# One ring of eight buffers for statistics and streamed units, spread in proportion to VectorE's passes

## The chip, the cores and the metric

The kernel runs on 1 core of one Trainium2 chip. The metric is device time in microseconds (us). TensorE is PE in the profile (its weight loads PEld), VectorE is DVE, ScalarE is ACT, GpSimd is POOL, SyncE is SP. "SPq" and "ACTq" are DMAs issued from the SP and ACT queues.

## The reference, cut to what matters

The input is one image of 16 channels of 2048 x 2048 floats. Both layers normalize over groups of two channels; the first adds a masked depthwise convolution, the second a bias that depends on row minus column and on the channel.

```
x = x + conv(gn(x))       # conv: 6 x 11 taps per channel, lower triangle (row >= column) in and out
x = x + (gn(x) + bias)    # bias[c, i, j] = table[i - j + 2047, c]; table from a small MLP
gn(v): mean and variance over 2 channels x 2048 x 2048, (v - m) / sqrt(var + 1e-5)
```

Above the diagonal the first layer changes nothing, so there the output is an affine function of the input plus the bias.

## The kernel before

A channel is four bands of 512 rows (128 partitions x 4 rows). A group is two channels; there are 8. The convolution runs over 90 tiles of a group (`NT` = 90), of which 42 touch the diagonal and take one more pass. The program is a pipeline of stages, one per group: in stage s, phase A takes the statistics of group s, phase B convolves group s-1, and phase C normalizes and stores group s-2. Stage 0 takes the first group's statistics alone, stage 1 has A and B, stages 2 to 7 have all three (stage 7 reads no statistics ahead for a next group), stage 8 has B and C, and stage 9 has C alone. Within a stage each engine walks the positions n = 0 to 89, one tile each, in an order written out by hand; an item "at position n" is issued between the tile work of n and of n + 1. SP has no tile work: it goes through its loads in the order of their positions, as fast as the waits of each let it.

Per position PE transposes a tile (L1117) and convolves one (L1131, 36 matmuls); ACT copies the transposed tile as f16 (L611), normalizes a later tile (L599) and sums squares of finished pieces (L631); DVE writes the f16 remainder (`split_lo`, L751), masks a diagonal tile (L764) and adds the result to x (`evict`, L766); POOL masks (L1031) and copies the halo columns (L1057, L1046). ACT and DVE work in order, so a late transfer for one item holds the tile work behind it.

Work around the tiles:

- **Statistics units ("a").** 58 units of 512 KB a group (`A_STREAM`) are loaded from x by SP (L488) into `abuf`, 4 buffers, and read by DVE: two `bn_stats` passes a unit (`stream_stats`, L779). Load `a` waits for `a_done` of unit `a - 4`. Loads lead their use by 2 positions.
- **Streamed units ("u").** 36 units of 512 KB a group (`STREAM`) are loaded from x, or from the output where the first layer's result was spilled there, by SP (L508) into `ubuf`, 4 buffers. Most are scaled by ACT (`scale_stream`, L658) and get the bias from POOL (`add_bias`, L1066); 13 take one DVE pass instead (`finish_stream`, L949). ACT issues the store (`store_stream`, L665) one position after a DVE unit and two after a POOL unit, and load `u` waits for the landing of store `u - 4`.
- **Kept blocks.** 14 parts of a group, in two halves each, stay in SBUF between B and C; DVE finishes them in place (L940), ACT stores them (L646), and SP loads the next group's into the same place (L524) once the store has landed.
- **Transit blocks** (`band`, 1 MB each) of bands 0 and 1 are loaded (L534), convolved and spilled (L638).
- The bias rows are loaded twice a group; the load for the second channel (position 43) waits for all units of the first.

A planner, `plan`, sets the positions. It books the fixed transfers in `traffic` (megabytes per position), and `spread` deals units over a window so that fixed and streamed traffic together come to the same level at each position, times `weight(n)`: 1 for statistics; `U_WEIGHT` for the u units: 1.8 below position 10, 1.5 above 82, else 1. After that a load is pushed back if its buffer would not be free, and with it the use:

```
p.u_load.append(max(at - 2, p.u_store[u - NUB] + 1) if u >= NUB else 0)
p.u.append(min(max(at, p.u_load[u] + 1, p.u[-1] if u else 0), hi))
p.a_load.append(max(at, p.a[a - NAB] + 1) if a >= NAB else at)
```

Of the kernel before, what the change touches and what calls it, by code (L numbers as in the profile page):

```python
# [25 lines left out]
def preact_conv_kernel(nc, x, wflip, w1, b1, w2, b2, w3, b3, out):  # L26
# [89 lines left out]
    def a_loads(g, a):  # L116

        of = lambda count: -(-(count - a % NAB) // NAB)
        return a // NAB + 1 + (of(NA0) + of(NA) * (g - 1) if g else 0)

# [3 lines left out]
    NAB, NUB = 4, 4  # L124
# [8 lines left out]

    U_WEIGHT = lambda n: 1.8 if n < 10 else 1.5 if n > 82 else 1.0
# [48 lines left out]
    def a_items(positions, s, n, do_a, do_next):  # L183

        if s == 0:
            return [(1, a) for a, at in enumerate(positions) if n == NT - 1 and at < 0]
        now = [(s, a) for a, at in enumerate(positions) if at == n]
        return (now if do_a else []) + [(s + 1, a) for a, at in enumerate(positions) if do_next and at == n - NT]

    def plan(do_a, do_b, do_c, on_dve=None):  # L190

        traffic = [0.0] * (NT + 8)
        lap = do_a and do_b and do_c

        def book(at, megabytes, over=2):
            for i in range(over):
                traffic[at + i] += megabytes / over
        for blk in KEPT:
            if do_c:
                book(kept_pos[blk][0] + 1, 1.0)  # L200
# [10 lines left out]
        def spread(count, megabytes, lo, hi, weight):  # L211
# [18 lines left out]
        p.u_load, p.u, p.on_dve, p.u_store, p.a_load, p.a = [], [], [], [], [], []  # L230
        if do_c:
            for c, (lo, hi) in enumerate(U_WINDOW):
                for at in spread(NU // 2, 1.0, lo, hi, U_WEIGHT if do_a else lambda n: 1.0):
                    u = len(p.u)
                    p.u_load.append(max(at - 2, p.u_store[u - NUB] + 1) if u >= NUB else 0)
                    p.u.append(min(max(at, p.u_load[u] + 1, p.u[-1] if u else 0), hi))
                    p.on_dve.append(on_dve[u] if on_dve else U_ON_DVE(p.u[u], u))
                    p.u_store.append(min(p.u[u] + (1 if p.on_dve[u] else 2), NT - 1))
                    book(p.u_load[u], 0.5, 1)
                    book(p.u_store[u], 0.5, 1)  # L240
        if lap:
            for at in spread(NA, 0.5, A_LO, A_END - 2, lambda n: 1.0):
                a = len(p.a)
                p.a_load.append(max(at, p.a[a - NAB] + 1) if a >= NAB else at)
                p.a.append(min(p.a_load[a] + 2, A_END))
        else:
            p.a_load, p.a = STEADY.a_load, STEADY.a
        return p
# [6 lines left out]
    N_DVE, N_POOL = u_before[1][NU], u_before[0][NU]  # L255

# [10 lines left out]
    with ctx:  # L267
# [15 lines left out]
        abuf = sb("abuf", [P, NAB, 2, BW], f32)  # L283
        ubuf = sb("ubuf", [P, NUB, 2, BW], f32)
# [38 lines left out]
        pos_in = ubuf[0:DIM, :, :, :].rearrange("p a b c -> p (a b c)")  # L323
# [21 lines left out]
        a_loaded = [sem(f"a_loaded{i}") for i in range(NAB)]  # L345
# [9 lines left out]
        u_loaded = [sem(f"u_loaded{i}") for i in range(NUB)]  # L355
# [3 lines left out]
        u_stored = [sem(f"u_stored{i}") for i in range(NUB)]  # L359
# [88 lines left out]
        def _(sp):  # L448
            def load_first():

                for i, (kind, of) in enumerate(FIRST_LOADS):
# [4 lines left out]
                    elif kind == "stream":  # L456
                        wait_alone(sp, a_done, max(0, of - NAB + 1))
                        sp.dma_start(unit_of(abuf, of % NAB, A_FIRST[of]), part(xv[A_FIRST[of][0], A_FIRST[of][1]], A_FIRST[of])
                                     ).then_inc(a_loaded[of % NAB], 16)
# [17 lines left out]
            def stage(s, do_a, do_b, do_c, do_next):  # L477
                p, ga, gb, gc = plan(do_a, do_b, do_c, on_dve), s, s - 1, s - 2
# [4 lines left out]
                for n in range(NT):  # L483
                    for g, a in a_items(p.a_load, s, n, do_a, do_next):
                        u = A_STREAM[a]

                        wait_alone(sp, a_done, a_base(g) + (a - NAB + 1 if a >= NAB else 0))
                        sp.dma_start(unit_of(abuf, a % NAB, u), part(xv[chan(g, u[0]), u[1]], u)  # L488
                                     ).then_inc(a_loaded[a % NAB], 16)
# [4 lines left out]
                    if do_a and s > 0:  # L494
                        if n == W_LOAD[0]:
                            load_taps(ga, 0)
                        load_transit(ga, 0, n)
                    if do_c:
                        for u in range(NU):
                            if p.u_load[u] == n:  # L500
                                c, b, q, nq = STREAM[u][:4]
                                wait_alone(sp, u_stored[u % NUB], 16 * (gc * (NU // NUB) + u // NUB))
                                spilled = q <= b
                                if spilled:
                                    for i in range(nq):
                                        wait_alone(sp, x1_spilled[(b, q + i)], 16 * (chan(gc, c) + 1))
                                src = (ov if spilled else xv)[chan(gc, c), b]
                                sp.dma_start(unit_of(ubuf, u % NUB, STREAM[u]), part(src, STREAM[u])  # L508
                                             ).then_inc(u_loaded[u % NUB], 16)
                        if n == BIAS_LOAD[1]:  # L510
                            load_bias(gc, 1)
                    if do_b:
# [4 lines left out]
                        if n == NEXT_BIAS_LOAD:  # L517
                            load_bias(gb, 0)

# [40 lines left out]
        def _(act):  # L560
# [93 lines left out]
            def scale_stream(g, u):  # L654

                v = ubuf[:, u % NUB, :, :]
                act.wait_ge(u_loaded[u % NUB], 16 * (g * (NU // NUB) + u // NUB + 1))
# [3 lines left out]
            def store_stream(g, u):  # L661
# [3 lines left out]
                act.dma_start(part(ov[chan(g, c), b], STREAM[u]), unit_of(ubuf, u % NUB, STREAM[u])  # L665
                              ).then_inc(u_stored[u % NUB], 16)

            def stage(s, do_a, do_b, do_c, do_next):
                p, ga, gb, gc = plan(do_a, do_b, do_c, on_dve), s, s - 1, s - 2
                for n in range(NT):  # L670
# [29 lines left out]
                    if do_c:  # L700
# [7 lines left out]
                        for u in range(NU):  # L708
                            if p.u[u] == n and not on_dve[u]:
                                scale_stream(gc, u)  # L710
# [4 lines left out]
                        for u in range(NU):  # L715
                            if p.u_store[u] == n:
                                store_stream(gc, u)
# [5 lines left out]
            for i in range(NUB):  # L723
                act.wait_ge(u_stored[i], 16 * G * (NU // NUB))
# [5 lines left out]
        def _(dve):  # L730
# [51 lines left out]
            def stream_stats(g, a):  # L782
                if a == 0:
                    wait(dve, s1_chain, 11 * g - 8)
                dve.wait_ge(a_loaded[a % NAB], 16 * a_loads(g, a))
                take_stats((A_STREAM if g else A_FIRST)[a], lambda q, r: abuf[:, a % NAB, q + r, :]).then_inc(a_done, 1)
# [156 lines left out]
            def finish_stream(g, u):  # L943
# [3 lines left out]
                dve.wait_ge(u_loaded[u % NUB], 16 * (g * (NU // NUB) + u // NUB + 1))  # L947
                v = unit_of(ubuf, u % NUB, STREAM[u])
# [11 lines left out]
            def stage(s, do_a, do_b, do_c, do_next):  # L960
                p, ga, gb, gc = plan(do_a, do_b, do_c, on_dve), s, s - 1, s - 2
                for n in range(NT):
# [17 lines left out]
                    if do_c:  # L980
# [6 lines left out]
                        for u in range(NU):  # L987
                            if p.u[u] == n and on_dve[u]:
                                finish_stream(gc, u)
                    for g, a in a_items(p.a, s, n, do_a, do_next):  # L990
# [19 lines left out]
        def _(pool):  # L1010
# [48 lines left out]
            def add_bias(g, u):  # L1059
# [5 lines left out]
                v = unit_of(ubuf, u % NUB, STREAM[u])  # L1065
                nc.gpsimd.tensor_tensor(v, v, bias_at(STREAM[u]), ALU.add).then_inc(u_added, 1)  # L1066

            def stage(s, do_a, do_b, do_c, do_next):
                p, ga, gb, gc = plan(do_a, do_b, do_c, on_dve), s, s - 1, s - 2
                for n in range(NT):  # L1070
# [15 lines left out]
                    if do_c:  # L1086
                        for u in range(NU):
                            if p.u[u] == n and not on_dve[u]:
                                add_bias(gc, u)
# [124 lines left out]
```

## Time and profile before

| | |
|---|---|
| median of 3 runs | 2722.15 us (2718.95 to 2722.83) |
| profiled execution | 2720.33 us, span 2718.5 us |
| busy share of the span | DVE 85%, PE 73%, ACT 61%, POOL 46% |
| moved by DMA | 901.17 MB, mean 331 GB/s |
| mean granted TensorE clock | 0.905 of full speed |

The span is the time from the first to the last instruction. "Busy" is the union of an engine's instructions. "DMA share" is the time of all packets over 16 engines' time; packets overlap a little, so it goes up to 1.04. A row "X <- Y" names who waited and what ended the wait.

### The profile page before, as it was taken

To read this page: it belongs to the slowest core of one execution; us is meant where nothing else is said; L and a number is where in the kernel's file an instruction comes from. 1 tells how busy PE (TensorE), PEld (TensorE's weight loads), DVE (VectorE), ACT (ScalarE), POOL (GpSimd) and SP (SyncE) were. 2 spreads that over 40 slices of the span, in tenths; PEclk is the share of its full clock that TensorE was granted. 3 is DMA by queue.
4 is the path that set the end of the run, shared out by engine and by line. 5 is a ranking of instruction groups with operands and counts; after the bars stand their busy time and mean duration, and the time that the engine had idled before them with its cause. 6 is when DMAs were issued, how large, how long until landed. Compare 5 with 4: busy or idle time off the path is not lost. (4 is left out here: it accounts for less than half of the span.)

```text
span 2718.5 us, 76785 instructions
## 1 busy us (share of the span) xinstructions
PE 1986.9 (73%) x28880; PEld 1885.9 (69%) x28880; DVE 2307.3 (85%) x4175; ACT 1661.5 (61%) x3051; POOL 1247.5 (46%) x1988
## 2 busy tenths in 40 slices
PE   4299978777787878877678777877768777989500
PEld 0199978777777767877678777777768777879400
DVE  7799988898889988899788998899888996969825
ACT  2177766756576656766567665666657665777521
POOL 1133254545445355544555455454544535655533
PEclk9999999998899989999889988999989998999855
DMA  9756569998899988999799998999889996979899
GB/s 338 274 197 201 192 216 408 357 374 313 325 409 353 367 326 339 399 348 359 293 394 384 353 353 303 405 365 371 323 330 401 354 358 222 351 269 344 303 337 347
DMA packets 316250, 901.17 MB, mean 331 GB/s; under 512 B 42416, under 2 KB 42416, under 8 KB 314000
## 3 DMA queue, kind: packets, MB, share of 16 engines
q1 hardware_dynamic: 199648, 579.79, 58.6%
q10 hardware_dynamic: 116416, 319.37, 30.6%
q8 instruction: 60, 0.98, 0.1%
q14 instruction: 126, 1.03, 0.1%
HBM read 579.50 MB, written 319.68 MB: 331 GB/s over the span
## 5 line engine op out<-in xcount | busy, mean ns | idle before, releaser
L1131 PEld LDWEIGHTS psY<-wsplit,XT 128*128 128x128 f16 x25920 | 1612.4, 102 | 313.7 <-DVE XT L751 116.5
L1131 PE MATMUL psY<-wsplit,XT 128*128 128x168 f16 (+5 forms) x25920 | 1638.1, 223 | 252.5 <-DVE XT L751 217.0
L611 ACT CAST XT<-psT 128x512 f16<-128x512 f32 x720 | 414.5, 576 | 534.6 <-PE psT L1117 316.4
L751 DVE TENSOR_TENSOR XT<-psT,XT 128x512 f16<-128x512 f32 x720 | 493.3, 685 | 191.8 <-ACT XT L611 190.0
L1031 POOL TENSOR_TENSOR xn<-xn,mask 128x512 f32<-128x512 f32 x336 | 440.6, 1311 | 423.4 <-ACT xn L599 364.4
L1117 PE MATMUL psT<-ident,xn 128*128 128x128 f32 x2880 | 486.9, 294 | 177.1 <-POOL xn L1031 136.7
L1066 POOL TENSOR_TENSOR ubuf<-ubuf,bias 128x1024 f32<-128x1024 f32 x184 | 413.5, 2248 | 375.6 <-ACT ubuf L658 375.1
L1057 POOL COPY halo<-XT 128x16 f16<-128x16 f16 x720 | 300.9, 418 | 611.9 <-DVE XT L751 598.9
L779 DVE BATCH_NORM_STATS2 entries<-abuf 128x6 f32<-128x512 f32 x872 | 549.0, 678 | 29.1 <-DMA abuf<-in_x 28.9
L1117 PEld LDWEIGHTS psT<-ident,xn 128*128 128x128 f32 x2880 | 321.8, 148 | 187.9 <-POOL xn L1031 121.6
L599 ACT ACTIVATE xn<-kept_c_band,normp 128x512 f32<-128x512 f32 (+2 forms) x496 | 398.4, 803 | 33.3 <-DMA kept_c_band<-in_x 17.0
L658 ACT ACTIVATE ubuf<-ubuf,outp 128x1024 f32<-128x1024 f32 x184 | 209.8, 1141 | 248.0 <-DMA ubuf<-in_x 147.7
L766 DVE SCALAR_TENSOR_TENSOR kept_c_band<-psY,wback,kept_c_band 128x472 f32<-128x472 f32 (+3 forms) x496 | 342.4, 690 | 16.5 <-PE psY L1131 9.9
L940 DVE SCALAR_TENSOR_TENSOR kept_c_band<-kept_c_band,outp,bias 128x1024 f32<-128x1024 f32 x224 | 339.0, 1521 | 11.7 <-ACT bias L651 11.7
L631 ACT ACTIVATE junk<-kept_c_band,cur 128x512 f32<-128x512 f32 (+2 forms) x464 | 311.4, 671 | 44.2 <-DVE kept_c_band L766 20.8
L949 DVE SCALAR_TENSOR_TENSOR ubuf<-ubuf,outp,bias 128x1024 f32<-128x1024 f32 x104 | 175.1, 1683 | 109.5 <-DMA ubuf<-in_x 73.4
L764 DVE TENSOR_TENSOR psY<-psY,mask 128x472 f32<-128x472 f32 (+2 forms) x336 | 202.6, 603 | 6.9 <-PE psY L1131 6.5
L599 ACT ACTIVATE xn<-band,normp 128x512 f32<-128x512 f32 (+1 forms) x224 | 174.2, 778 | 26.9 <-DVE normp L860 26.9
L1046 POOL COPY XT<-halo 128x16 f16<-128x16 f16 x720 | 151.1, 210 | 46.0 <-PE psY L1131 41.9
L766 DVE SCALAR_TENSOR_TENSOR band<-psY,wback,band 128x472 f32<-128x472 f32 (+2 forms) x224 | 150.1, 670 | 5.7
L631 ACT ACTIVATE junk<-band,cur 128x512 f32<-128x512 f32 x192 | 132.0, 688 | 29.7 <-DVE band L766 20.2
L631 ACT ACTIVATION_READ_ACCUMULATOR junk<-kept_c_band,cur 128x1 f32 x464 | 87.1, 188 | 0.0
(78 smaller groups left out, 464.1 us busy)
## 6 DMA issues: line engine op xcount, KB each, us to landing
abuf<-in_x SPq DMA_DIRECT2D x436, 512.0 KB, 8.1
out<-ubuf ACTq DMA_DIRECT2D x288, 512.0 KB, 6.2
kept_c_band<-in_x SPq DMA_DIRECT2D x224, 512.0 KB, 8.5
out<-kept_c_band ACTq DMA_DIRECT2D x224, 512.0 KB, 6.9
ubuf<-in_x SPq DMA_DIRECT2D x192, 512.0 KB, 7.1
band<-in_x SPq DMA_DIRECT2D x48, 1024.0 KB, 9.1
out<-band ACTq DMA_DIRECT2D x48, 1024.0 KB, 9.9
ubuf<-out SPq DMA_DIRECT2D x96, 512.0 KB, 8.6
```

Source lines behind the costliest of these rows:

```text
L599: last = nc.scalar.activation(to[:, :, 0:whole, :], slot(c, b)[:, :, x0:x0 + XC * whole].rearrange("p k (i c) -> p k i c", c=XC), ACT.Iden ...
L611: nc.scalar.copy(XT[:, n % NB3, 0, :, 2:P + 2], psT[n % NB3][:, :, :]).then_inc(hi_ready, 1)
L631: nc.scalar.activation(junk[:, 0:nr * (c1 - c0)].rearrange("p (r c) -> p r c", r=nr), slot(c, b)[:, r:r + nr, BW * q + c0:BW * q + c1], AC ...
L751: nc.vector.tensor_tensor(XT[:, n % NB3, 1, :, 2:P + 2], psT[n % NB3][:, :, :], XT[:, n % NB3, 0, :, 2:P + 2], ALU.subtract).then_inc(lo_r ...
L766: nc.vector.scalar_tensor_tensor(out=xs, in0=y, scalar=col(wback, c), in1=xs, op0=ALU.mult, op1=ALU.add, accum_out=sums[:, n:n + 1]).then_ ...
L779: last = nc.vector.bn_stats(entries[:, e, :], row(q, r))
L940: nc.vector.scalar_tensor_tensor(out=v, in0=v, scalar=col(outp, 0), in1=bias_at(blk, nr // 2 * h, nr // 2), op0=ALU.mult, op1=ALU.add).the ...
L1031: nc.gpsimd.tensor_tensor(v, v, m, ALU.mult).then_inc(xn_ready, 1)
L1057: nc.gpsimd.tensor_copy(halo[:, t, :, :, :], XT[:, n % NB3, :, :, P:P + 2]).then_inc(halo_out, 1)
L1066: nc.gpsimd.tensor_tensor(v, v, bias_at(STREAM[u]), ALU.add).then_inc(u_added, 1)
L1117: last = nc.tensor.transpose(psT[m][:, i, :], xn[:, m, i, :, :].rearrange("p k c -> p (k c)"), ident[:, :])
L1131: last = nc.tensor.matmul(psY[m][:, 0:rows, o + lo_c:o + hi_c], XT[:, m, xp, i, 2 - sh:2 - sh + P], wsplit[:, c, wp, K * sh:K * sh + rows, ...
```

## The change

`abuf` and `ubuf` become one tensor `ring` of eight buffers. All loads of both kinds, over all groups, are put into one list sorted by wanted position, and the k-th takes buffer k mod 8, whichever kind it is. A load waits for what its buffer held last: `a_done` if that was a statistics unit, the landing of the store if it was a streamed unit. A load that its buffer pushes back pushes back all loads behind it. The lead of a u load grows from 2 to 3 positions, and to 14 in the last group; a statistics load keeps its lead of 2.

The weights of `spread` change for both kinds: `lasts[n]` is the mean number of VectorE passes at positions n - 2 to n + 2 over the stage's mean, where `passes` counts the tile work, the diagonal pass, kept blocks, early statistics and the weights' building. Positions with many such passes get more of both kinds. `U_ON_DVE` is unchanged; by the new positions it gives 11 units to DVE and 25 to POOL, where it gave 13 and 23.

```diff
-    NAB, NUB = 4, 4
+    NAB, NRING = 4, 8
-    U_WEIGHT = lambda n: 1.8 if n < 10 else 1.5 if n > 82 else 1.0
+    def passes(do_a, do_b, do_c):
+        work = [1.0] * NT
+        for n, (c, b, t) in enumerate(TILES):
+            at = (n + 1) % NT
+            work[at] += 1.0 + is_diag[n]
+        for at in [at for pos in kept_pos.values() for at in pos]:
+            work[at] += 2.0 * do_c
+        for at in EARLY_STATS:
+            work[at] += 2.0 * do_a
+        for at in [W_BUILD[0]] * do_a + [W_BUILD[1]] * do_b:
+            work[at] += 3.0
+        return work
...
+        work = passes(do_a, do_b, do_c)
+        mean = sum(work) / NT
+        lasts = [sum(work[(n + i) % NT] for i in range(-2, 3)) / (5 * mean) for n in range(NT)]
...
-                return max(0.02, level * weight(n) - smooth[n])
+                return max(0.02, level * lasts[n % NT] - smooth[n])
...
+                for at in spread(NU // 2, 1.0, lo, hi):
+                    p.on_dve.append(on_dve[len(p.u)] if on_dve else U_ON_DVE(at, len(p.u)))
+                    p.u.append(at)
...
+            p.a = spread(NA, 0.5, A_LO, A_END - 2)
...
+    A_LEAD, U_LEAD, LAST_LEAD = 2, 3, 14
+    wanted = [(max(NT * g + at, NT - 1), "a", g, a) for g in range(1, G) for a, at in enumerate(STEADY.a)]
+    for g in range(G):
+        p = plan(g + 2 < G, g + 1 < G, True, on_dve)
+        lead = U_LEAD if g + 1 < G else LAST_LEAD
+        wanted += [(NT * (g + 2) + max(at - lead, 0), "u", g, u) for u, at in enumerate(p.u)]
+    wanted.sort()
...
+    for k, (at, kind, g, i) in enumerate(wanted):
+        key, n = (kind, g, i), k % NRING
+        load = max(at, load, free_at[n])
+        buffer_of[key], held_by[key], in_buffer[n] = n, in_buffer[n], key
...
+        if kind == "a":
+            use[kind] = min(max(load + A_LEAD, use.get(kind, 0)), NT * g + A_END)
+            free_at[n] = use[kind] + 1
+        else:
+            use[kind] = max(NT * (g + 2) + planned[(g, i)], load + A_LEAD, use.get(kind, 0))
+            stored = min(use[kind] + (1 if on_dve[i] else 2), NT * (g + 3) - 1)
+            free_at[n] = stored + 1
...
-        abuf = sb("abuf", [P, NAB, 2, BW], f32)
-        ubuf = sb("ubuf", [P, NUB, 2, BW], f32)
+        ring = sb("ring", [P, NRING, 2, BW], f32)
...
+            def load_unit(key, u, src):
+                kind, g, i = key
+                n, held = buffer_of[key], held_by[key]
+                if held and held[0] == "a":
+                    wait_alone(sp, a_done, a_base(held[1]) + held[2] + 1)
+                elif held:
+                    wait_alone(sp, u_stored[n], 16 * store_count[held])
+                sp.dma_start(unit_of(ring, n, u), part(src[chan(g, u[0]), u[1]], u)).then_inc(ring_loaded[n], 16)
```

The engines' loops take their units from the tables of this walk (`loads_at`, `uses_at`, `stores_at`) in place of `a_items` and the plan's own lists. The order within a position is as before: on SP statistics loads, transit loads, u loads, kept loads; on DVE tile work, kept blocks, u units, statistics. In stage 1 the first eight statistics units of group 1 are used at position 1 and the next six at position 4; before, ten were used at the last position of stage 0.

## Rows read from the trace of the kernel before

**Rows 1.** The page: busy engines and DMA totals.

```profile
PE 1986.9 (73%) x28880; PEld 1885.9 (69%) x28880; DVE 2307.3 (85%) x4175; ACT 1661.5 (61%) x3051; POOL 1247.5 (46%) x1988
...
DMA packets 316250, 901.17 MB, mean 331 GB/s; under 512 B 42416, under 2 KB 42416, under 8 KB 314000
```

**Rows 2.** Windows: stages 4, 7, 8 and 9.

```profile
core 0: us, PE busy (x) PEld busy (x) DVE busy (x) ACT busy (x) POOL busy (x), PEclk, DMA share, GB/s
...
1012.30:1333.10 320.80, 247.54 (x3606) 236.92 (x3606) 284.30 (x522) 205.62 (x381) 157.80 (x247) 0.93 0.95 357
...
1974.20:2292.30 318.10, 246.67 (x3606) 236.14 (x3606) 276.44 (x506) 205.38 (x380) 159.16 (x247) 0.92 0.91 342
2292.30:2550.20 257.90, 225.39 (x3539) 219.17 (x3540) 203.63 (x362) 196.21 (x363) 151.00 (x238) 0.98 0.85 307
2550.20:2718.50 168.30, 3.52 (x57) 3.33 (x54) 78.13 (x72) 35.16 (x38) 56.10 (x24) 0.52 0.92 337
```

**Rows 3.** Windows: stage 4 in stretches, from positions 0, 9, 15, 27, 42, 58, 76.

```profile
1012.30:1053.90 41.60, 30.33 (x408) 28.55 (x409) 34.74 (x72) 22.15 (x40) 21.77 (x27) 0.86 0.79 289
1053.90:1075.30 21.40, 16.34 (x240) 15.90 (x238) 16.59 (x29) 13.12 (x26) 8.86 (x17) 0.91 1.04 409
1075.30:1113.30 38.00, 33.16 (x511) 32.03 (x510) 37.04 (x69) 26.10 (x49) 16.92 (x33) 0.96 1.03 416
1113.30:1161.00 47.70, 37.28 (x570) 36.05 (x568) 36.64 (x72) 35.55 (x66) 28.81 (x43) 0.95 0.98 379
1161.00:1215.30 54.30, 44.83 (x640) 42.48 (x640) 53.88 (x99) 34.41 (x62) 24.89 (x46) 0.91 0.97 341
1215.30:1281.70 66.40, 50.00 (x739) 47.52 (x737) 61.34 (x109) 42.38 (x77) 25.02 (x45) 0.95 0.97 368
1281.70:1333.10 51.40, 35.60 (x520) 34.38 (x517) 44.07 (x84) 31.91 (x65) 31.53 (x43) 0.91 0.90 327
```

**Rows 4.** Waits of DVE and ACT in stage 4.

```profile
DVE XT L751 <- ACT XT L611: 21.5, 11, 5.9
DVE ubuf L949 <- DMA ubuf<-in_x: 5.5, 3, 3.1
DVE entries L779 <- DMA abuf<-in_x: 4.8, 1, 4.8
DVE ubuf L949 <- DMA ubuf<-out: 1.3, 2, 1.1
...
ACT ubuf L658 <- DMA ubuf<-in_x: 16.5, 7, 4.9
...
ACT ubuf L658 <- DMA ubuf<-out: 7.6, 3, 5.3
```

**Rows 5.** Timeline of ACT and DVE at position 13 of stage 4.

```profile
1070.10 1.15 ACT L658 ACTIVATE ubuf<-ubuf,outp 128x1024 f32<-128x1024 f32 x1 [4.72 <-DMA ubuf<-in_x]
...
1071.75 0.69 DVE L751 TENSOR_TENSOR XT<-psT,XT 128x512 f16<-128x512 f32 x1 [3.89 <-ACT XT L611]
```

**Rows 6.** The page: costs of the moved passes.

```profile
L1066 POOL TENSOR_TENSOR ubuf<-ubuf,bias 128x1024 f32<-128x1024 f32 x184 | 413.5, 2248 | 375.6 <-ACT ubuf L658 375.1
...
L779 DVE BATCH_NORM_STATS2 entries<-abuf 128x6 f32<-128x512 f32 x872 | 549.0, 678 | 29.1 <-DMA abuf<-in_x 28.9
...
L949 DVE SCALAR_TENSOR_TENSOR ubuf<-ubuf,outp,bias 128x1024 f32<-128x1024 f32 x104 | 175.1, 1683 | 109.5 <-DMA ubuf<-in_x 73.4
```

**Rows 7.** The page: DMA issues, size, us to landing.

```profile
abuf<-in_x SPq DMA_DIRECT2D x436, 512.0 KB, 8.1
out<-ubuf ACTq DMA_DIRECT2D x288, 512.0 KB, 6.2
```

**Rows 8.** Timeline of PE at the start of stage 1.

```profile
133.50 3.78 PE L1131 MATMUL psY<-wsplit,XT 128*128 128x148 f16 x36 [5.15 <-DVE XT L751]
```

**Rows 9.** Chain of waits in the tail: start, us, what.

```profile
2677.57 8.14 DMA out<-ubuf
2685.87 4.40 DMA ubuf<-out
```

More of the change, by code:

```diff
@@ L255, in preact_conv_kernel, with units_at @@
     N_DVE, N_POOL = u_before[1][NU], u_before[0][NU]
+    A_LEAD, U_LEAD, LAST_LEAD = 2, 3, 14
+    planned = {}
+    wanted = [(max(NT * g + at, NT - 1), "a", g, a) for g in range(1, G) for a, at in enumerate(STEADY.a)]
+    for g in range(G):
+        p = plan(g + 2 < G, g + 1 < G, True, on_dve)
+        lead = U_LEAD if g + 1 < G else LAST_LEAD
+        planned.update({(g, u): at for u, at in enumerate(p.u)})
+        wanted += [(NT * (g + 2) + max(at - lead, 0), "u", g, u) for u, at in enumerate(p.u)]
+    wanted.sort()
+    loads_at, uses_at, stores_at = {}, {}, {}
+    buffer_of, load_count, store_count, held_by = {}, {}, {}, {}
+    in_buffer = [("a", 0, max(range(i, NA0, NAB))) if i < NAB else None for i in range(NRING)]
+    loads = [len(range(i, NA0, NAB)) if i < NAB else 0 for i in range(NRING)]
+    stores = [0] * NRING
+    free_at = [0] * NRING
+    for a in range(NA0):
+        buffer_of[("a", 0, a)], load_count[("a", 0, a)] = a % NAB, a // NAB + 1
+    load, use = 0, {}
+    for k, (at, kind, g, i) in enumerate(wanted):
+        key, n = (kind, g, i), k % NRING
+        load = max(at, load, free_at[n])
+        buffer_of[key], held_by[key], in_buffer[n] = n, in_buffer[n], key
+        loads[n] += 1
+        load_count[key] = loads[n]
+        loads_at.setdefault(load, []).append(key)
+        if kind == "a":
+            use[kind] = min(max(load + A_LEAD, use.get(kind, 0)), NT * g + A_END)
+            free_at[n] = use[kind] + 1
+        else:
+            hi = U_WINDOW[CPG * i // NU][1]
+            use[kind] = max(NT * (g + 2) + planned[(g, i)], load + A_LEAD, use.get(kind, 0))
+            assert use[kind] <= NT * (g + 2) + hi
+            stored = min(use[kind] + (1 if on_dve[i] else 2), NT * (g + 3) - 1)
+            stores_at.setdefault(stored, []).append(key)
+            stores[n] += 1
+            store_count[key] = stores[n]
+            free_at[n] = stored + 1
+        uses_at.setdefault(use[kind], []).append(key)
+        assert load < use[kind]
+    def units_at(table, kind, s, n):
+        return [key for key in table.get(NT * s + n, []) if key[0] == kind]
     xv = x.rearrange("o c (b p k) w -> (o c) b p k w", p=P, k=K)
@@ L344, in preact_conv_kernel @@
         scale_chain = sem("scale_chain")
-        a_loaded = [sem(f"a_loaded{i}") for i in range(NAB)]
+        ring_loaded = [sem(f"ring_loaded{i}") for i in range(NRING)]
         a_done = sem("a_done")
@@ L358, in preact_conv_kernel @@
         u_finished = sem("u_finished")
-        u_stored = [sem(f"u_stored{i}") for i in range(NUB)]
+        u_stored = [sem(f"u_stored{i}") for i in range(NRING)]
         kept_done = sem("kept_done")
@@ L483, in stage @@
                 for n in range(NT):
[L484 to L489, printed above, removed]
+                    for key in units_at(loads_at, "a", s, n):
+                        load_unit(key, A_STREAM[key[2]], xv)
                     if do_b:
@@ L497, in stage @@
                         load_transit(ga, 0, n)
-                    if do_c:
[L499 to L509, printed above, removed]
+                    for key in units_at(loads_at, "u", s, n):
+                        c, b, q, nq = STREAM[key[2]][:4]
+                        spilled = q <= b
+                        if spilled:
+                            for i in range(nq):
+                                wait_alone(sp, x1_spilled[(b, q + i)], 16 * (chan(key[1], c) + 1))
+                        load_unit(key, STREAM[key[2]], ov if spilled else xv)
+                    if do_c:
                         if n == BIAS_LOAD[1]:
@@ L707, in stage @@
                             shift_bias(gc, 1, NV)
-                        for u in range(NU):
-                            if p.u[u] == n and not on_dve[u]:
-                                scale_stream(gc, u)
+                        for _, g, u in units_at(uses_at, "u", s, n):
+                            if not on_dve[u]:
+                                scale_stream(g, u)
                         for blk in KEPT:
@@ L714, in stage @@
                                     store_kept(gc, blk, h)
-                        for u in range(NU):
-                            if p.u_store[u] == n:
-                                store_stream(gc, u)
+                        for _, g, u in units_at(stores_at, "u", s, n):
+                            store_stream(g, u)
             stages(stage)
@@ L722, in _ @@
                 act.wait_ge(half_stored, 16 * G)
-            for i in range(NUB):
-                act.wait_ge(u_stored[i], 16 * G * (NU // NUB))
+            for i in range(NRING):
+                act.wait_ge(u_stored[i], 16 * stores[i])
             for s in x1_spilled.values():
@@ L986, in stage @@
                                     finish_kept(gc, blk, h)
[L987 to L990, printed above, removed]
+                        for _, g, u in units_at(uses_at, "u", s, n):
+                            if on_dve[u]:
+                                finish_stream(g, u)
+                    for _, g, a in units_at(uses_at, "a", s, n):
                         stream_stats(g, a)
@@ L1086, in stage @@
                     if do_c:
-                        for u in range(NU):
-                            if p.u[u] == n and not on_dve[u]:
-                                add_bias(gc, u)
+                        for _, g, u in units_at(uses_at, "u", s, n):
+                            if not on_dve[u]:
+                                add_bias(g, u)
             stages(stage)
```

65 lines of the change are left out of this document (25 added, 40 removed).

## The prediction

> **What bounds the kernel now.** I read the page first: DVE is the busiest engine, and the DMA engines moved 331 GB/s on average [rows 1]. A kernel in stages has to be read by stage, so I cut the span into windows where DVE starts tile 2 of each group [rows 2]. Stages 2 to 7 are six of a kind, of which 4 and 7 stand here (320.8 and 318.1 us): in stage 4 DVE is busy for 284.3 of 320.8 us, PE for 247.5, and the DMA share is 0.95. So DVE leads, with 36.5 us of idle time a stage, and the DMA is close behind. Stage 8 is mostly PE's (225.4 of 257.9 us). In stage 9 no engine is busy for half of the 168.3 us, and the DMA share is 0.92.
>
> Then I cut stage 4 into stretches of positions [rows 3]. The idle time of DVE (window less busy) is 6.9, 4.8, 1.0, 11.1, 0.4, 5.1 and 7.3 us. The first belongs to the chain of the second layer's statistics at position 1, which the change leaves alone. The rest is late data: DVE waits for u loads and for a statistics load itself (5.5, 1.3 and 4.8 us), and mostly for ACT's f16 copy, 21.5 us, because ACT stands waiting for a u load, 24.1 us [rows 4]. At position 13 it can be seen: ACT waits 4.72 us for a u load, and DVE 3.89 us for ACT [rows 5]. Loads are late around positions 13, 30 to 41, 58 and 78 to 87.
>
> The same windows show how full the DMA is. From position 9 to 26 its share is 1.03 to 1.04 and it moves 409 to 416 GB/s: this is its limit. From 42 to 75 the share is 0.97 at only 341 and 368 GB/s. Only 0 to 8 (0.79) and 76 to 89 (0.90) have real room.
>
> **The change part by part.** I worked the plan's arithmetic through for a steady stage, old and new, and counted units by the same stretches. Statistics uses, before and after: 6 and 10 (positions 0 to 8), 1 and 2 (9 to 14), 9 and 6 (15 to 26), 9 and 4 (27 to 41), 14 and 14 (42 to 57), 10 and 14 (58 to 75), 9 and 8 (76 to 89). DVE's u units: 1 and 0, 0 and 1, 1 and 1, 3 and 3, 1 and 1, 1 and 2, 6 and 3, in all 13 and 11. Transfers of 0.52 MB (statistics loads, u loads, u stores), with 9 to 26 as one stretch: 14 and 15, 18 and 23, 30 and 18, 18 and 23, 19 and 29, 31 and 22.
>
> Costs: a statistics unit is 549.0 / 436 = 1.26 us of DVE, a u unit on DVE 1.68 us; a POOL unit costs POOL 2.25 us [rows 6]. POOL has half of each stage idle [rows 2], so its two more units a group are free; if that cover were gone they would cost 4.5 us. The change therefore does this, per stretch, against the windows of [rows 3]:
>
> 0 to 8: four statistics units come, one DVE unit goes: +5.0 - 1.7 = +3.3. The one new wait here: the statistics load for position 8 takes a buffer from which a POOL unit is stored at position 5, so it waits for a store and then a load, 6.2 + 8.1 = 14.3 us [rows 7], where three short positions lie between. I take 1 us (0 to 5). Together +4.
>
> 9 to 26: +1.3 + 1.7 - 3.8 = -0.8 for DVE, and the wait at 13 shrinks with the longer lead, perhaps by 2. But five more transfers, 2.6 MB, enter a stretch that is at its limit. At 413 GB/s that is 6.3 us. Some can arrive late, since the next stretch gets light. Between -3 and +6 I take +2.
>
> 27 to 41: DVE loses five statistics units, 6.3 us, and 12 transfers leave. DVE would be busy for 30.3 us, but PE is busy for 37.3 here, so PE becomes the bound and the stretch can't fall below that. I take 39.5 for 47.7: -8. The idle time of DVE that is left here is then PE's.
>
> 42 to 57: DVE's work is the same. Four statistics loads want positions 48 to 50, but one takes the buffer of a u unit stored at 49 and holds the other three behind it: all four are used at 52. I take 1.5 us (0 to 3). Five more transfers, 2.6 MB at 0.97 share.
>
> 58 to 75: +5.0 + 1.7 = +6.7 for DVE, waits of 2 (three loads at 70 and 71 again wait for stores, 0 to 5), and ten more transfers, 5.2 MB. By DVE the two stretches grow by 10. By DMA: they moved 42.9 MB in 120.7 us at 0.97, so at a share of 1.03 they could move 377 GB/s, and 42.9 + 7.8 MB need 134.5 us: +14; the five and ten transfers are planned places, and some will land in the next stretch. The wait at 58 stays: its load stands in SP's queue behind a kept load, and both are where they were. I take +11 for 42 to 75.
>
> 76 to 89: -1.3 - 5.0 = -6.3 for DVE, and the waits here, 7.3 us, should fall to 1.5, since seven u units stand where twelve stood: -12.
>
> Sum: 4 + 2 - 8 + 11 - 12 = -3 us a stage. The same sum by DVE and PE alone, with none of the DMA's surcharges, is 4 - 3 - 8 + 10 - 12 = -9, or -7 if the wait at 13 stays; with the upper ends of the new waits and of the DMA, +6. Six stages: -18 (from -42 to +36).
>
> A rule of the Trainium skill speaks against any gain here. The page "DMA: Bandwidth & Descriptors", section "Where 436 GB/s comes from", has it that for transfers between HBM and SBUF the HBM share of a core, about 358 GB/s, binds. By it a stage of 320.8 us x 357 GB/s = 114.5 MB couldn't take less than 320 us. [Rows 3] show 409 and 416 GB/s over 59 us together, so the limit that binds in this trace lies higher, and it is the stretches, not the mean, that I go by.
>
> Stage 1: ten statistics units stood between the f16 remainders of tiles 1 and 2, and PE waited 5.15 us for that [rows 8]. Now eight stand one position later, when PE has three tiles to go on with. -3 (0 to -5). Stage 8: two DVE passes fewer, 3.4 us, but PE leads; -2 (0 to -5).
>
> Stage 9: the chain runs store, load, pass, store, load: each buffer goes around alone, 8.14 us for a store and 4.40 for the load that waited for it [rows 9]. Eight buffers and loads 14 positions ahead keep more under way, also across the second bias load, which now has five units of the second channel loaded ahead of its wait. The bytes stay: at a share of 1.00 in place of 0.92 the 168.3 us become 155, and at 1.04, 149. Filling and emptying the pipeline stay, so I take 159: -9 (-3 to -14).
>
> Total: -18 - 3 - 2 - 9 = -32. The profiled execution took 2720.33 us, so 2688; the median of the runs shown lies 1.8 us above it: 2690.
>
> **The rivals.** (1) DVE's sum holds. The plan gives more traffic to positions that last long, so the surcharges of the DMA don't come: -7 a stage, 2720 - 42 - 14 = 2664, 2666 by the median. For it: the mean share of 0.95 leaves 5 to 8% unused. Against: 42 to 75 is full already. (2) The DMA keeps its rate: what 27 to 41 and 76 to 89 give, 42 to 75 takes back; 0 a stage, 2708. The skill's figure above gives nearly this, 2700. (3) Slower: statistics are chained to stores. Before, a statistics load waited only for DVE's own earlier pass; now about half wait for the landing of a store, and SP holds everything behind such a load. If the loads used at 8, 21 to 25, 52 and 69 to 73 cost 13.5 of their upper ends' 18 us (5, 5, 3 and 5), where the sum has 4.5, a stage is 6 us longer: 2722 + 36 - 14 = 2744. It decides from 3.2 us a stage on: (5.4 + 14) / 6. (4) PE's stretch is worse than its busy time: the clock granted there was 0.95, and with PE the bound each gap in its chain counts. It would add 2 to 3 us a stage: 2705, within (2).
>
> **How the numbers follow.** Forecast (2670 to 2706) 0.45; rival 1 0.20; rivals 2 and 4 0.17; rival 3 0.15; the change does nothing because waits simply move, 0.03. Within 0.2% (5.4 us) can't be told from no change. Faster: 0.45 + 0.20 + 0.11 of rivals 2 and 4 = 0.76; same 0.08; slower 0.16. The range goes from 2650, which leaves out a few hundredths of rival 1 with no new wait at all, to 2728, which leaves out rival 3.
>
> **What would show it.** Windows by the same positions: 27 to 41 near 39 us with PE busy for most of it; 76 to 89 near 39; 58 to 75 above 75 with a share near 1.03; ACT's waits for u loads below 10 us a stage; DVE's waits for statistics loads up from 4.8 us, at positions 8, 52, 58 and 72. Stage 9 below 162 us with a share of 0.97 or more. The prediction is wrong if 42 to 75 doesn't grow by 10, or if ACT's waits stay at 24 us because SP's queue, not the buffers, made the loads late.

## The result

The changed kernel takes 2744.9 us (median of 4 runs, 2742.7 to 2750.2) against 2722.3: a ratio of 1.0088, 95% interval 1.0071 to 1.0106. It is slower by 0.9%. The forecast was 2690, with a range to 2728.

Windows of the profile after, stages 4, 7, 8 and 9 (columns as in [rows 2]):

```profile
1026.70:1352.80 326.10, 249.04 (x3606) 237.68 (x3606) 280.98 (x522) 207.71 (x381) 160.79 (x250) 0.91 0.93 351
2004.80:2328.20 323.40, 249.45 (x3606) 238.16 (x3606) 273.93 (x506) 206.95 (x380) 159.52 (x249) 0.91 0.89 335
2328.20:2589.60 261.40, 226.02 (x3508) 220.34 (x3509) 200.37 (x361) 196.75 (x362) 155.26 (x238) 0.97 0.81 301
2589.60:2744.40 154.80, 5.09 (x88) 4.83 (x85) 82.67 (x68) 38.53 (x44) 66.74 (x29) 0.53 0.95 369
```

Against [rows 2]: stage 4 takes 326.1 us, not 320.8, although DVE is busy for 3.3 us less; stage 8 takes 3.5 us more; stage 9 takes 13.5 us less. The six steady stages together are 30.4 us longer (from the start of stage 2 to that of stage 8: 1955.1 after, 1924.7 before), and stage 2 starts 5.5 us later. 5.5 + 30.4 + 3.5 - 13.5 = 25.9 us, the difference of the spans.

Stage 4 after in the same stretches of positions as [rows 3]:

```profile
1026.70:1071.10 44.40, 32.17 (x441) 30.78 (x442) 37.55 (x79) 21.39 (x37) 20.00 (x28) 0.85 0.69 249
1071.10:1093.70 22.60, 15.95 (x243) 14.60 (x241) 18.05 (x34) 13.79 (x25) 9.54 (x14) 1.00 1.04 401
1093.70:1133.90 40.20, 32.45 (x460) 30.83 (x461) 36.12 (x65) 28.44 (x51) 22.82 (x33) 0.92 1.02 396
1133.90:1176.90 43.00, 37.71 (x584) 36.73 (x580) 30.56 (x62) 33.21 (x64) 22.95 (x40) 0.96 0.94 367
1176.90:1231.90 55.00, 43.85 (x638) 42.13 (x637) 53.31 (x97) 35.28 (x63) 26.62 (x47) 0.91 0.98 350
1231.90:1310.70 78.80, 52.69 (x735) 49.58 (x732) 68.42 (x116) 44.56 (x79) 31.02 (x48) 0.89 1.00 386
1310.70:1352.80 42.10, 34.23 (x522) 33.05 (x520) 36.97 (x81) 31.05 (x64) 27.84 (x43) 0.95 0.85 304
```

Read the sixth row first. Positions 58 to 75 take 78.8 us where they took 66.4. DVE has 7.1 us more to do there, but it is also idle for 10.4 us in place of 5.1, and the DMA share is 1.00. The fourth and the last row are what was bought for that: 27 to 41 falls by 4.7 us, and 76 to 89 by 9.3.

What DVE waits for in stage 4 after (us in total, times, longest):

```profile
DVE entries L823 <- DMA ring<-in_x: 22.3, 8, 5.2
DVE XT L795 <- ACT XT L654: 14.9, 10, 5.9
```

Beside [rows 4]: the waits for ACT fell from 21.5 to 14.9 us, and the statistics loads, late once in this stage before, are late eight times. ACT's own waits for loads:

```profile
ACT xn L642 <- DMA kept_c_band<-in_x: 16.2, 5, 5.5
...
ACT ring L702 <- DMA ring<-in_x: 14.2, 5, 6.4
ACT ring L702 <- DMA ring<-out: 6.2, 3, 3.2
```

Its waits for streamed units are 20.4 us, for 24.1 before, and its waits for kept blocks 16.2, for 3.3. Over stages 2 to 7 the first are 132.5 us, for 133.2 before, and the second 93.1, for 17.0: the longer lead did not bring ACT's loads earlier. What SP waited for in stage 4, first before, then after:

```profile
SPq L405 <- DVE entries L779: 72.5, 17, 18.5
SPq L405 <- DMA out<-ubuf: 72.0, 16, 10.3
SPq L405 <- DMA out<-kept_c_band: 59.2, 16, 11.6
```

```profile
SPq L446 <- DMA out<-ring: 176.2, 29, 15.3
SPq L446 <- DMA out<-kept_c_band: 20.9, 7, 12.9
...
SPq L446 <- DVE entries L823: 14.1, 1, 14.1
```

SP now waits for stores of streamed units for 176 of 326 us. All its waits together are hardly longer than before (242 us for 238, with the rows not shown): what changed is what it waits for, and which loads stand behind. Position 10 shows one late load: a wait of SP before it, its issue by SP, the time to its landing, and DVE's wait.

```profile
SPq L446 <- DMA out<-ring: 12.3, 1, 12.3
```

```profile
1063.95 1.11 SPq L561 DMA_DIRECT2D ring<-in_x  x1
```

```profile
ring<-in_x SPq DMA_DIRECT2D x1, 512.0 KB, 13.2
```

```profile
1077.15 1.29 DVE L823 BATCH_NORM_STATS2 entries<-ring 128x6 f32<-128x512 f32 x2 [3.43 <-DMA ring<-in_x]
```

SP's wait of 12.3 us for a store ended at about 1059.4 us. Two ring loads and two kept loads went first, and the statistics unit of position 10 left at 1063.95. It took 13.2 us to land, where 8.6 is the median of these loads in the whole run; the DMA share was 1.02 to 1.04 while it was under way. DVE stood 3.43 us for it. So SP's wait for a store and the full DMA can both have a part in this wait, and which weighs more isn't shown.

### The profile page after: what moved, and what is told of

It reads as the page before. It is cut to its first block and busy times, and to the rows that moved or that the text cites. A ratio compares the mean times of both kernels' runs of the same rounds, so it can differ in the third digit from the quotient of the medians.

```text
span 2744.4 us, 76787 instructions
## 1 busy us (share of the span) xinstructions
PE 1983.5 (72%) x28880; PEld 1876.1 (68%) x28880; DVE 2285.4 (83%) x4159; ACT 1679.0 (61%) x3067; POOL 1274.9 (46%) x2004
## 3 DMA queue, kind: packets, MB, share of 16 engines
q14 instruction: 126, 1.03, 0.1%
## 5 line engine op out<-in xcount | busy, mean ns | idle before, releaser
L823 DVE BATCH_NORM_STATS2 entries<-ring 128x6 f32<-128x512 f32 x872 | 548.5, 678 | 130.5 <-DMA ring<-in_x 130.5
L1112 POOL TENSOR_TENSOR ring<-ring,bias 128x1024 f32<-128x1024 f32 x200 | 459.9, 2301 | 397.1 <-ACT ring L702 397.1
L1163 PE MATMUL psT<-ident,xn 128*128 128x128 f32 x2880 | 479.9, 291 | 123.2 <-POOL xn L1077 69.2
L1103 POOL COPY halo<-XT 128x16 f16<-128x16 f16 x720 | 265.2, 368 | 648.2 <-DVE XT L795 639.5
L642 ACT ACTIVATE xn<-kept_c_band,normp 128x512 f32<-128x512 f32 (+2 forms) x496 | 398.3, 803 | 148.8 <-DMA kept_c_band<-in_x 93.1
L985 DVE SCALAR_TENSOR_TENSOR kept_c_band<-kept_c_band,outp,bias 128x1024 f32<-128x1024 f32 x224 | 350.7, 1573 | 17.0 <-ACT bias L694 17.0
L702 ACT ACTIVATE ring<-ring,outp 128x1024 f32<-128x1024 f32 x200 | 227.7, 1141 | 217.8 <-DMA ring<-in_x 98.2
L1092 POOL COPY XT<-halo 128x16 f16<-128x16 f16 x720 | 163.5, 227 | 68.0 <-PE psY L1177 64.3
L995 DVE SCALAR_TENSOR_TENSOR ring<-ring,outp,bias 128x1024 f32<-128x1024 f32 x88 | 137.1, 1558 | 62.3 <-DMA ring<-in_x 46.4
```

The lines of the kernel that those rows point to most:

```text
L642: last = nc.scalar.activation(to[:, :, 0:whole, :], slot(c, b)[:, :, x0:x0 + XC * whole].rearrange("p k (i c) -> p k i c", c=XC), ACT.Iden ...
L823: last = nc.vector.bn_stats(entries[:, e, :], row(q, r))
L985: nc.vector.scalar_tensor_tensor(out=v, in0=v, scalar=col(outp, 0), in1=bias_at(blk, nr // 2 * h, nr // 2), op0=ALU.mult, op1=ALU.add).the ...
L1103: nc.gpsimd.tensor_copy(halo[:, t, :, :, :], XT[:, n % NB3, :, :, P:P + 2]).then_inc(halo_out, 1)
L1163: last = nc.tensor.transpose(psT[m][:, i, :], xn[:, m, i, :, :].rearrange("p k c -> p (k c)"), ident[:, :])
```

## The experiments

Each kernel ran beside the kernel before on the same chip, and its ratio is to those runs; the kernel before took 2718.9 to 2722.3 us in the medians. The stretches are means over stages 2 to 6, from the starts of DVE's L751 (in the changed kernels its line moves with the edits); "transfers" and "passes" are the plan's 0.52 MB transfers and statistics units at positions 58 to 75.

| kernel | us | ratio (95%) | transfers, passes 58-75 | 0-8 | 9-26 | 27-41 | 42-57 | 58-75 | 76-89 |
|---|---|---|---|---|---|---|---|---|---|
| before | 2722 | 1 | 19, 10 | 41.8 | 60.7 | 45.9 | 54.4 | 66.7 | 51.9 |
| the change | 2744.9 | 1.0088 (1.0071 to 1.0106) | 29, 14 | 44.3 | 63.1 | 42.4 | 55.8 | 78.7 | 42.0 |
| e1: lead 3 | 2731.8 | 1.0046 (1.0026 to 1.0065) | 29, 14 | 42.8 | 64.4 | 43.2 | 55.7 | 76.2 | 40.6 |
| e2: two rings | 2724.2 | 1.0021 (1.0007 to 1.0034) | 29, 14 | 43.9 | 63.5 | 40.7 | 53.8 | 77.6 | 41.3 |
| e3: old spread | 2644.9 | 0.9722 (0.9692 to 0.9752) | 20, 9 | 40.1 | 60.7 | 48.1 | 53.5 | 63.9 | 47.0 |
| e4: first free | 2703.8 | 0.9943 (0.992 to 0.9966) | 29, 14 | 43.5 | 61.2 | 41.1 | 53.8 | 78.3 | 40.7 |
| e5: new spread, statistics | 2755.5 | 1.0123 (1.0101 to 1.0145) | 28, 19 | 45.1 | 65.5 | 42.0 | 58.5 | 75.8 | 42.2 |
| e6: new spread, units | 2709.5 | 0.9962 (0.9948 to 0.9976) | 20, 3 | 40.6 | 56.3 | 54.3 | 50.6 | 64.5 | 53.5 |
| e7: old spread, two rings | 2713.3 | 0.997 (0.9956 to 0.9985) | 19, 9 | 40.3 | 62.8 | 47.8 | 55.0 | 62.7 | 52.1 |
| e8: old spread, first free | 2630.7 | 0.9675 (0.9655 to 0.9695) | 20, 9 | 39.9 | 60.4 | 46.7 | 54.2 | 62.6 | 46.4 |
| e9: half the passes | 2687.8 | 0.9883 (0.9849 to 0.9918) | 29, 14 | 41.2 | 63.0 | 42.9 | 52.6 | 80.3 | 38.9 |
| e10: half the bytes | 2675.0 | 0.9837 (0.9813 to 0.986) | 29, 14 | 44.0 | 58.8 | 40.2 | 55.9 | 73.8 | 42.0 |
| e11: e8 and lead 3 | 2617.0 | 0.962 (0.9593 to 0.9647) | 20, 9 | 40.9 | 55.2 | 50.4 | 55.0 | 60.5 | 45.8 |
| e12: e4 and lead 3 | 2708.4 | 0.9949 (0.9932 to 0.9965) | 29, 14 | 45.2 | 61.9 | 41.0 | 55.8 | 74.1 | 41.2 |

**e1, the lead.**

```diff
-    A_LEAD, U_LEAD, LAST_LEAD = 2, 3, 14
+    A_LEAD, U_LEAD, LAST_LEAD = 3, 3, 14
```

> The change with one number altered: a statistics unit is used 3 positions after its load, not 2; ring, spread and the loads' order stay. Chaining theory (the loads are late because their buffers wait for stores and SP holds the rest behind them): a position is worth some 3.5 us, so the eight waits of DVE for statistics loads in stage 4, 22.3 us, should fall to about 8, and the total from 2745 to about 2725. Spread theory (the new places fill the DMA where it is already full): loads come as late as they come, waits move to ACT's own loads; 2738 to 2748. If lead is all there is to it: at or below 2715.

DVE's waits for statistics loads in stage 4 fall from 22.3 to 3.0 us, more than expected, and yet the total falls by only 13, to between the two theories' figures. DVE's waits for ACT rise from 14.9 to 24.6, because ACT now waits longer for its own loads: 39.0 us for streamed units in stage 4, for 20.4 in the change. The lateness moved to the next engine.

**e2, two rings of four.**

```diff
-        key, n = (kind, g, i), k % NRING
-        load = max(at, load, free_at[n])
+        key, n = (kind, g, i), (NAB if kind == "u" else 0) + count[kind] % NAB
+        count[kind] += 1
+        load = last[kind] = max(at, last.get(kind, 0), free_at[n])
```

> The change with the eight buffers split again, four for statistics and four for streamed units, each kind with its own order; the new spread, the lead of 3 and DVE's 11 units stay. Chaining theory: statistics loads no longer wait for stores; a stage falls from 326 to 316 to 320 us, stage 1 gives back 5, and stage 9 loses its gain again (155 to about 166): total 2700 to 2720. Spread theory: stages stay at 324 to 328, stage 9 loses 10, total 2745 to 2755.

Between the two theories: stage 4 falls to 320.6, but no further, and stage 9 goes up to 177.5. Positions 58 to 75 hardly move (77.6). DVE still waits 19.7 us for statistics loads in stage 4, for 22.3 in the change. Their buffers wait for no store now, but SP issues them in one order with the streamed units' loads, and stands before stores for those for 90.8 us.

**e3, the old weights with the new ring.** `spread` gets its `weight` back, `U_WEIGHT` for units and 1 for statistics.

> The change with the old weights of the spread (1 for statistics; 1.8, 1 and 1.5 for streamed units) and the new ring of eight; DVE has 13 units again. Spread theory: stages fall back to 321 or below, stage 9 keeps its gain of 13: total 2700 to 2712. Chaining theory: statistics loads still wait for stores, now most around positions 30 to 50 and 77 to 89 where the old spread has its streamed units; stages 325 to 330, total 2740 to 2765.

This is the verdict on the spread with the ring of eight: 100 us less than the change, and far below what either theory gave. 27 to 41 and 76 to 89 get longer again, by 5.7 and 5.0 us; 58 to 75 alone gives 14.8 us a stage, and the other three 9. The window of that stretch in stage 4 of this kernel, to be read beside the sixth row above:

```profile
1197.20:1261.80 64.60, 49.80 (x721) 47.34 (x719) 61.93 (x107) 41.30 (x76) 25.57 (x45) 0.92 0.99 379
```

Nearly the same rate and share, 6 MB less (24.5 for 30.4).

**e4, the buffer that is free the longest.**

```diff
-        key, n = (kind, g, i), k % NRING
+        key = (kind, g, i)
+        n = min(range(NRING), key=lambda j: free_at[j])
```

> The change with another choice of buffer: each load takes the buffer that is free the longest by the plan, not number k mod 8. Of 58 statistics loads 20 still follow a store in their buffer, but only two within two positions of it (the change: 24, and seven within two). Chaining theory: DVE's waits for statistics loads fall to about 10 us a stage, stages to 320 to 322, total 2712 to 2728. Spread theory: no change from 2745 by more than 5.

41 us gained, more than expected, with nothing changed but which load waits for whom. So the fixed rotation has a real cost, but not by DVE's waits alone: those for statistics loads in stage 4 only fall to 19.5 us, not to 10. Over stages 2 to 7 they fall from 129.9 to 107.0, and ACT's waits for streamed and kept loads from 225.6 to 133.4. 58 to 75 stays at 78.3.

**e5 and e6, the new weights for one kind each.**

```diff
-                for at in spread(NU // 2, 1.0, lo, hi):
+                for at in spread(NU // 2, 1.0, lo, hi, U_WEIGHT if do_a else lambda n: 1.0):   # e5; lasts in e6
-            p.a = spread(NA, 0.5, A_LO, A_END - 2)
+            p.a = spread(NA, 0.5, A_LO, A_END - 2, lambda n: lasts[n % NT])                    # e5; 1 in e6
```

> Ring of eight, old weights for the streamed units, the change's weights for the statistics alone. Of a steady stage's 58 statistics uses 19 then stand at positions 58 to 75 and 2 at 27 to 41, with 28 and 19 transfers. Theory A (the statistics' weights are the loss: they move VectorE's passes to where VectorE is the bound and away from where TensorE is): as slow as the change or slower, 2740 to 2780, stretch 58 to 75 above 80 us. Theory B (the units' weights are the loss): 2650 to 2680.

> Ring of eight, the change's weights for the streamed units, weight 1 for the statistics, which the planner deals last and around the units: 15 uses at 27 to 41, 3 at 58 to 75, 18 at 76 to 89; transfers 29, 20 and 32. Theory A: near the kernel with the old spread and the ring, 2640 to 2670, since what counts is how much of VectorE's work stands in the long stretches. Theory B: slow, 2720 to 2760.

e5's total came out in theory A's range, e6's in neither: 2709.5. The planner deals statistics last and around the units, so one kind alone doesn't have the change's places. For 58 to 75 theory A's reason is contradicted: e5 has five passes more there than the change and takes 75.8 us, not above 80, and e6 has six passes fewer than e3 and takes 64.5 for 63.9. The four kernels go by their transfers: 29 and 28 against 20 and 20. In e6 76 to 89 carries 18 statistics units, and there DVE is busy for 50.1 of 54.3 us in stage 4. So there are two ways to lose: transfers where the DMA is full, and passes where DVE would then be the bound. 27 to 41 is long in e6 as well (54.3), with 29 transfers and 15 passes; its window in stage 4 has DVE busy for 44.2 of 55.7 us and a DMA share of 0.97, and which of the two holds it isn't shown. Stage 8 tells the kinds apart: 248.3 us in e5 as in e3 (248.0), 262.0 in e6 as in the change (261.4). Its loss is the units' weights.

**e7, the old spread with two rings**, which leaves of the change only the leads and an earlier start of stage 1, there with four statistics units at a time. (In e6, e7 and e11 a unit's use is also kept within its window where its load would push it out by a position.)

> The old spread with four buffers for each kind and the lead of 3: the kernel before but for the lead and stage 1. If the ring of eight is what gains in the kernel with the old spread (2645): 2710 to 2725, with ScalarE's and VectorE's waits for units at 78 to 87 as in the kernel before, and stage 9 at 168 to 178. If the gain is from the lead: 2650 to 2670.

As expected for the ring: 2713.3 against e3's 2644.9. The ring of eight is worth 68 us under the old spread. In the profiled executions it is 70: 7.4 us in each steady stage, 9.8 in stage 8 and 21.9 in stage 9, less 6.1 before stage 2.

With e2, e3 and the change this makes a square (us of a steady stage, mean of stages 2 to 7):

| | old spread | new spread |
|---|---|---|
| two rings of four | 319.7 (e7) | 320.0 (e2) |
| ring of eight, k mod 8 | 312.2 (e3) | 325.9 (the change) |

With two rings the new spread costs next to nothing in a steady stage, and 11 us in the whole: 58 to 75 grows by 14.9 us as it does with the ring, but 27 to 41 and 76 to 89 give back 7.1 and 10.8. The ring under the old spread has by itself brought 76 to 89 from 52.1 to 47.0, so there is less left for the spread to gain. And the ring, worth 7.4 us a stage under the old spread, costs 5.9 under the new one. The two parts of the change spoil each other.

**e8, the old spread, the ring, the first free buffer.** The edits of e3 and e4 together.

> The old spread, the ring, and each load in the buffer that is free the longest by the plan, not number k mod 8. With the change's spread this choice gained 41 us (2745 to 2704). If the chaining of loads to stores costs the same under the old spread: 2645 less 20 to 40, 2605 to 2625. If the long stretches were what made a late store count, so that little is left: 2635 to 2650.

14 us less than e3, a third of what the same choice gave under the new spread. It came out below the range for "little is left" and above the one for "the same cost": 2630.7.

**e9 and e10, half of the passes and half of the bytes**, on the changed kernel.

```diff
-                take_stats(..., lambda q, r: ring[:, i, q + r, :])
+                take_stats(..., lambda q, r: ring[:, i, q + r, 0:8 if q + r else BW])   # e9
...
+                if kind == "a":                                                          # e10
+                    to, of = (to[:, 0:1, :], of[:, 0:1, :]) if u[5] == 2 else (to[:, :, 0:BW], of[:, :, 0:BW])
...
-                take_stats(..., lambda q, r: ring[:, i, q + r, :])
+                take_stats(..., lambda q, r: ring[:, i, 0 if g else q + r, :])          # e10
```

> The change with half of the statistics passes taken out: of the two passes over a statistics unit from the ring the second reads 8 columns in place of 512 (its statistics are left out of the computation so). All transfers stay. VectorE saves some 0.55 us a unit, 32 us a stage, 8 us at positions 58 to 75. If VectorE's passes are what makes 58 to 75 long (78.7 us): it falls to 70 to 72. If the DMA is: it stays at 76 or above.

> The change with half of the bytes of the statistics units taken out: each load from group 1 on brings 256 KB in place of 512, and both passes read that half (the other half is left out of the statistics). VectorE's passes stay. 15 MB of 114 MB a stage go, some 3.5 MB of 30 at positions 58 to 75. If the DMA makes that stretch long: from 78.7 to 70 to 72 us, VectorE's busy time of 68 us being the floor. If VectorE's passes do: 76 or above.

58 to 75 in stage 4, e9, then e10:

```profile
1190.90:1274.50 83.60, 53.87 (x715) 50.85 (x712) 61.78 (x118) 44.15 (x79) 28.75 (x48) 0.84 0.97 378
```

```profile
1204.90:1279.70 74.80, 51.56 (x743) 48.61 (x741) 68.96 (x118) 44.13 (x79) 31.76 (x48) 0.91 0.96 355
```

With 6.6 us of DVE's work gone the stretch is not shorter at all (80.3 in the mean, for 78.7): DVE only waits more. With bytes gone it falls by 4.9, less than the 7 to 9 expected. The DMA makes it long, and DVE with its 68 us is the next bound close behind. Elsewhere passes count too: e9 is 3.1 us shorter at 0 to 8, 3.2 at 42 to 57 and 3.1 at 76 to 89, and a steady stage gains 7.2 us by it; e10 gains 11.9. In stage 1 only the passes count: stage 2 starts at 354.7 us in e9 and at 375.0 in e10, for 373.1 in the change and 367.6 before.

**e11 and e12, lead 3 and first free under either spread.**

> Old spread, ring, buffer that is free the longest (2631), and a lead of 3 positions for statistics too. If what is left of VectorE's waits for statistics loads is a matter of lead: 2612 to 2625. If the wider lead only holds buffers longer, so that the streamed units' loads are later: 2628 to 2645.

> The change with the buffer that is free the longest and a lead of 3 for statistics, and its own spread: the same two edits that brought the old spread from 2645 to 2617. If the spread's cost is transfers put where the DMA is full, these edits can't take it away: 2675 to 2695, with 58 to 75 still at 75 us or more. If the cost was late loads after all: 2640 or below, with 58 to 75 near 68.

e11 is the fastest kernel here, 2617.0 us. e12 is at 2708.4, above its range and no better than e4: with the new spread the lead brings nothing more. The same two edits on either spread leave 91 us between them, so with a ring of eight most of the spread's cost isn't late loads that a better choice of buffers could bring forward. 58 to 75 came to 74.1, just under the 75 named.

## Why the prediction was wrong

By the steady stage, in us, prediction against the means of the table (after less before):

| stretch | predicted | measured |
|---|---|---|
| 0 to 8 | +4 | +2.5 |
| 9 to 26 | +2 | +2.4 |
| 27 to 41 | -8 | -3.5 |
| 42 to 75 | +11 | +13.5 |
| 76 to 89 | -12 | -9.8 |
| stage | -3 | +5.1 |

**The terms that failed** are "27 to 41: -8" first, then the +11 and the -12. Every one of the three was wrong to the same side. For 27 to 41 I started from 47.7 us in stage 4, while the mean over five stages is 45.9; and I let the stretch fall nearly to PE's busy time, 39.5 for 37.3. It fell to 42.4, with loads late in it: DVE is busy for 30.6 of 43.0 us there, as I had it, but it waits 7.4 us for loads itself. e2, where the buffers of statistics loads wait for no store, has 40.7: so chaining took back about two of the missing microseconds. For 76 to 89 I had DVE's waits fall from 7.3 to 1.5 us as late data. No load is late for DVE there any more, but it still stands 4.5 us for ACT, and its idle time is 5.1. The gains of a light stretch I had written in full and its new waits at nothing.

**The premise behind them failed as well.** I had ACT's waits for streamed units below 10 us a stage, and named as a sign of being wrong that they stay at 24 because SP's queue, not the buffers, makes the loads late. They are 20.4 us in stage 4 and 22.1 in the mean of stages 2 to 7, as before (22.2), with 15.5 more for kept blocks, for 2.8 before. The kept blocks' loads take no buffer of the ring and stand only in SP's queue; in e4 another choice of ring buffers takes the waits for them from 15.5 to 6.9 us a stage. So the queue passes waits on to loads that have nothing to do with the ring.

For 42 to 75 I had both numbers, +10 by DVE and +14 by the DMA at its limit, and took +11 on the ground that some transfers would land in the next stretch. It was +13.5: the larger of the two bounds was nearly it, and not a mean of them. (That +14 fits so well is partly luck: stage 4 moved 6.7 MB more there, not 7.8, at a share of 0.98 and 1.00, not 1.03.) By the plan nine more transfers than in e3 cost 14.8 us at 58 to 75, 1.6 us each. By the windows of stage 4 it is 5.9 MB more in 14.2 us more, 418 GB/s. e9 and e10 show that it is the bytes.

**The mechanism of rival 3 was there.** Its 2744 us is what was measured, but as a sum of other parts, so that the number is met by luck. The fixed rotation costs 41 us by e4, and the shared ring 43 outside stage 9 by e2 (21 in the whole, and 22.7 that e2 loses in stage 9). Under the old spread the same rotation costs 14 (e8), and the shared ring gains. Its places were half right: late loads at 10, 22, 29, 31, 58 and 67, and none at 52. I had a price for it and a threshold (3.2 us a stage) that the measured +5.1 passed, and gave it 0.15. The trace of before spoke for more: SP was waiting for most of a stage already (the three rows of before above make 204 of 321 us), so a load behind it had little slack left. Rival 4, a lower clock in PE's stretch, can be left out: the granted clock at 27 to 41 was 0.96, for 0.95 before.

**Stage 1**: -3 predicted, +5.5 measured. The wait of PE that was to go did not go: PE waits once for 5.6 us there, for 5.15 before. Eight units at position 1 and six at position 4 come with the ring, under the old spread too (e3, with the same 5.6 us of wait). In e7 it is four at a time; PE's wait is 1.1 us, and stage 2 starts at 363.3, 4.3 us earlier than before. The ring adds 6.1 us to that (e3) and the spread 3.7. Halving DVE's passes takes 18.4 us off (e9), so that it is they that hold stage 1 up. **Stage 8**: -2 predicted, +3.5 measured, by the units' weights (e5, e6); why its places cost 13 us against the old ones stays open. **Stage 9**: -9 predicted, -13.5 measured. That the ring would shorten it was right, and the size too small. The share rose from 0.92 to 0.95 only, where I had 0.97 or more; but the rate rose from 337 to 369 GB/s, so that more was moved at the same share, and why is not shown. The ring does it, not the longer lead: with two rings and that lead it took 174.6 and 177.5 us.

**What was right**: that 42 to 75 was full and would pay for the rest, that POOL's two more units are free (ACT's waits for POOL's halo copies in stage 4 are 14.8 us after and 14.6 before), and that the waits at the end of a stage would shrink, though by less than I had. The rule of the Trainium skill's page "DMA: Bandwidth & Descriptors", section "Where 436 GB/s comes from", that about 358 GB/s binds between HBM and SBUF, doesn't hold in these traces, with one core running: 416 GB/s in 38 us of a stage before, and in 54.9 us of e11:

```profile
1027.00:1081.90 54.90, 48.47 (x734) 47.44 (x732) 53.23 (x97) 38.00 (x73) 27.37 (x47) 0.94 1.03 416
```

## What to carry to other kernels

Spreading transfers "where a position lasts long" assumes that the length of a position is given. Here it was partly the DMA's own doing, and what was added there cost its full transfer time, while the stretches that were relieved did not fall all the way to their next bound; sum each stretch as the larger of its bounds, with a price for its new waits, and only then across stretches.

Test a change that does two things with each of them alone: the ring with its leads was worth 2.8% (e3), the spread with two rings changed a steady stage by 0.3 us, and together they were 0.9% slower. When buffers of two kinds are shared, choose the buffer by when it comes free, since a fixed rotation ties a kind that is released by its reader to one that is released only by a landed store, and an in-order queue passes that wait on to everything behind it.

## What was not expected of the hardware

At a DMA share of about 1.0 the rate was not one number: 350 GB/s at 0.98 (the change, 42 to 57), 386 at 1.00 (58 to 75), 416 at 1.03 (e11, 9 to 26). What sets it isn't shown. It isn't the 1 MB blocks: each of the three windows has three of their transfers. The first also has the second channel's bias rows and four loads of taps of 31.5 KB in it. A mean rate or a mean share of a stage, 0.93 after, tells little of which stretch is full.
